# Reordering each quarter of the feed-forward groups: scaling and split first, statistics, normalisations and softmax of the other groups later

## The chip, the cores and the metric

The kernel runs on one core of a Trainium2 chip. The metric is the device time of one execution in microseconds (us). Beside it stands the span, from the first to the last instruction of one profiled execution.

Five engines work side by side, each with its own queue of instructions that it takes strictly in order: PE (TensorE, matrix products and transposes; its weight loads are listed as PEld), DVE (VectorE), ACT (ScalarE), POOL (GpSimd) and SP (SyncE, which here only issues DMAs). They wait for one another by semaphores. An instruction that waits holds up everything behind it on its own engine.

## The reference, cut to what matters

The input is 2048 tokens of 1024 numbers. Three stages follow each other; the first and the third are the feed-forward stage, with the same weights, and the middle one is a convolution with blockwise attention, which the change doesn't touch.

```
def ffn(x, weight, bias, gate_w, in_channel_scale, out_channel_scale):
    routing = softmax(x @ gate_w.T)                  # 8 experts
    in_scale = routing @ in_channel_scale
    out_scale = routing @ out_channel_scale
    return x * in_scale @ sign(weight).T * out_scale + bias

x = x + 0.5 * ffn(layernorm(x), ...)
x = x + attention(layernorm(x), ...)
x = x + 0.5 * ffn(layernorm(x), ...)
```

## The kernel before

The feed-forward stage is one function, `ffn_phase`, called twice: turn 1 (about 0 to 250 us) and turn 2 (about 905 us to the end). It takes the tokens in eight groups of 256. The body of the loop is run once per group g, and is cut into four quarters q = 0 to 3; each quarter makes one 128x512 tile of the group's output. Each engine has its own body, written out by hand, and in it work of several groups is interleaved:

- Group g itself: PE makes the product with the signed weights, sixteen matmuls a quarter (L638, `product`, two halves of eight), and the output scale (L626, `out_scale`); ACT copies the output scale (L543); DVE multiplies product and scale into y (L469, called the output multiply here); POOL adds residual and bias (L267, L270).
- Group g+1, two of its eight chunks k a quarter: PE makes the input scale of a chunk (L621, `in_scale`), DVE multiplies it with the transposed tokens (L343, `scale`), ACT rounds the result to its high part (L504, `high`), DVE subtracts to get the low part (L348, `low`). There are only two PSUM banks for these chunks, so the `in_scale` of chunk k waits for the `low` of chunk k-2. In a quarter, PE's second `in_scale` stands between the two halves of the product. In quarter 0 the first one is followed by the logits.
- Group g+2: logits (L597) and their way back (L604) in quarter 0, softmax on DVE (L319 to L336) with its exponential on ACT (L495) in quarter 1, its transposition on PE (L610, `routing`) and copy on ACT (L499) in quarter 3.
- Group g+3: statistics on DVE (L296 to L305, `stats`), the inverse root on POOL (L241, `power`) and the normalisation on DVE (L310, `normalise`) in quarter 0; its four transposes on PE (L587) in quarters 1, 2, 3 and 3, with copies on ACT (L487).
- Group g-1, in turn 1 only: statistics of its output on DVE (L356 to L365, `out_stats`) and the inverse root on POOL (L263) in quarter 0, normalisation on DVE (L371, `out_normalise`) in quarter 2, and in quarter 3 four rounds of transposes on PE (L654, `normed`) and copies on ACT (L516, `copy_normed`), which share one PSUM bank and so take turns.

In quarter 0, DVE before does the statistics of g+3 and of g-1, then the two scalings and the first split of g+1, then the normalisation of g+3, then the output multiply. Groups 0 and 5 to 7 are special: group 0 has no g-1; groups 5 to 7 have no g+3; groups 6 and 7 have no g+2; in group 7 of turn 1 POOL and DVE also prepare filters of the convolution (L785, L792).

Of the kernel before, what the change touches and what calls it, by code (L numbers as in the profile page):

```python
# [13 lines left out]
ALU = mybir.AluOpType  # L14
# [58 lines left out]
def exists(g):  # L73

    return not isinstance(g, int) or 0 <= g < NG
# [5 lines left out]
def ffn_phase(nc, sems, set_up, turn, src, dst, w_t, bias, gate_t, ics, ocs, ident, X, conv):  # L81
# [33 lines left out]
    with ExitStack() as ctx:  # L115
# [55 lines left out]
        with nc.Block() as block:  # L171
# [58 lines left out]
            def _(pool):  # L230
# [27 lines left out]
                def body(g, p):  # L258
                    if exists(g + 3):
                        power(g + 3)  # L260
                    if X is not None and exists(g - 1):
                        pool.wait_ge(n_var, g)
                        pool.tensor_tensor(nrstd[:], nvpe[:], minus_half[:], ALU.pow).then_inc(n_rstd, 1)  # L263
                    for q in range(4):
                        t, h = q // 2, slice(q % 2 * HALF, q % 2 * HALF + HALF)
                        pool.wait_ge(res_loaded[t], 16 * g + 16)
                        pool.tensor_tensor(res[:, t, h], res[:, t, h], hbias[:, h], ALU.add).then_inc(res_biased, 1)  # L267
                        pool.wait_ge(res_biased, 4 * g + q + 1)
                        pool.wait_ge(m_scaled, 4 * g + q + 1)
                        pool.tensor_tensor(y[:, p, t, h], y[:, p, t, h], res[:, t, h], ALU.add).then_inc(y_done, 1)  # L270
                        if q == 3 and X is not None and exists(g - 1) and not late(g):
                            differences(g - 1)
                        if q == 0 and X is not None and late(g):
                            conv.outer_sum(pool, 0)
                            conv.outer_sum(pool, 1)
                        if q >= 2 and X is not None and late(g):
                            t = q - 2
                            pool.wait_ge(n_var, NG + t)
                            pool.tensor_tensor(nrstd[:, t:t + 1], nvpe[:, t:t + 1], minus_half[:, t:t + 1], ALU.pow).then_inc(n_rstd, 1)
# [4 lines left out]
            def _(dve):  # L284
# [148 lines left out]

                def body(g, p):
                    for q in range(4):
                        if q == 0 and exists(g + 3):
                            stats(g + 3, 1 - p)
                        if q == 0 and X is not None and exists(g - 1):
                            out_stats(g - 1, 1 - p)
                        if exists(g + 1):  # L440
                            scale(g + 1, 1 - p, 2 * q)
                            if q:
# [1 line left out]
                            scale(g + 1, 1 - p, 2 * q + 1)  # L444
                            low(g + 1, 1 - p, 2 * q)
                        if q == 0 and exists(g + 3):
                            normalise(g + 3, 1 - p)
                        if q == 1 and exists(g + 2):
                            softmax(g + 2)
                        if q == 2 and X is not None and exists(g - 1):  # L450
                            out_normalise(g - 1, 1 - p)
                        if q == 3 and exists(g + 1):
                            low(g + 1, 1 - p, KD - 1)
                        if q == 2 and X is not None and late(g):
# [26 lines left out]
            def _(act):  # L481
# [15 lines left out]
                def copy_routing(g, p):  # L497
                    act.wait_ge(r_full, g + 1)
                    act.copy(rT[:, p, :], p_r[:, 0:FTOK]).then_inc(r_copied, 1)  # L499
# [39 lines left out]
                def body(g, p):  # L539
                    for q in range(4):  # L540
# [5 lines left out]
                        if q == 0 and X is not None and late(g):  # L546
                            conv.outer_scale(act, 0)
                            conv.outer_scale(act, 1)
                        if q == 3 and exists(g + 2):
                            copy_routing(g + 2, p)  # L550
                        if q == 0 and exists(g + 2):
                            copy_logits(g + 2)
                        if exists(g + 1):
                            high(g + 1, 1 - p, 2 * q)
                        if q == 3 and X is not None and exists(g - 1):
                            copy_normed(g - 1, 0)
                            copy_normed(g - 1, 1)
                        if exists(g + 1):
                            high(g + 1, 1 - p, 2 * q + 1)
                        if q == 3 and X is not None and exists(g - 1):  # L560
                            copy_normed(g - 1, 2)
                            copy_normed(g - 1, 3)
                        if q == 1 and exists(g + 2):
                            exponent(g + 2)
                        if exists(g + 3):
                            for piece in PIECES[q]:
# [8 lines left out]
            def _(pe):  # L575
# [99 lines left out]
                def body(g, p):  # L675
                    for q in range(4):
# [7 lines left out]
                            routing(1)  # L684
                        if exists(g + 1):
                            in_scale(g + 1, 1 - p, 2 * q)
                        if q == 3 and exists(g + 2):
                            routing(g + 2)
                        if q == 0 and exists(g + 2):
                            logits(g + 2, p)  # L690
                        if q == 3 and X is not None and exists(g - 1):
                            for c in range(4):
                                normed(g - 1, 1 - p, c)
                                product(g, p, q, 2 * c, 2 * c + 2)
                                if c == 1 and exists(g + 1):
                                    in_scale(g + 1, 1 - p, 2 * q + 1)
                                if c == 1 and exists(g + 3):
                                    transposes(g + 3, 1 - p, 2)
                        else:
                            if not first:  # L700
                                product(g, p, q, 0, 4)
                            if exists(g + 1):
                                in_scale(g + 1, 1 - p, 2 * q + 1)
                            if q == 3 and exists(g + 3):
# [978 lines left out]
```

## Time and profile before

| | |
|---|---|
| device time, median of 3 runs | 1110.57 us (1109.88 to 1112.51) |
| the profiled execution, its own time | 1117.16 us |
| its span | 1115.4 us |
| PE busy | 952.7 us, 85% |
| DVE busy | 718.2 us, 64% |
| ACT busy | 452.8 us, 41% |
| POOL busy | 371.6 us, 33% |

In the page, busy shares are means over the whole span. The stages differ, so the timeline (every instruction in order of its start, with the engine's idle time before it and what released it) and the table by stretches are what tells about the feed-forward groups.

### The profile page before, as it was taken

What the parts mean: (1) busy time and instruction counts of PE and PEld (TensorE: products, weight loads), DVE (VectorE), ACT (ScalarE), POOL (GpSimd) and SP (SyncE); (2) the same over time, 40 slices, a digit from 0 to 9 for tenths busy, and PEclk for the clock granted to TensorE, in tenths of its full rate; (3) what the DMA queues carried; (4) which work ended last, traced back from release to release, by engine and by line L of the source; (5) the groups of instructions that cost most, each with busy time, mean ns of one, the idle gap of its engine ahead of it and who ended that gap; (6) DMA issues with size and microseconds to landing.
All of it is one profiled execution on the core that took longest, in us unless ns stands there. A gap on an engine that the chain in (4) does not pass through costs nothing. (4 is left out here: it accounts for less than half of the span.)

```text
span 1115.4 us, 15622 instructions
## 1 busy us (share of the span) xinstructions
PE 952.7 (85%) x4960; PEld 716.4 (64%) x4960; DVE 718.2 (64%) x1469; ACT 452.8 (41%) x1127; POOL 371.6 (33%) x305
## 2 busy tenths in 40 slices
PE   4898888868898998967978996998799746999997
PEld 3576666653335876845766785886678634678786
DVE  6677775477998885532774587288458447576652
ACT  3534444431244352323763454356345305433431
POOL 2245555564542200000223131133214411355555
PEclk9799999988999999986988997998899885999999
DMA  8333322322323426533002112121101258154243
GB/s 280 127 133 114 113 75 76 132 95 85 113 94 135 168 66 245 207 133 113 2 19 76 39 57 76 38 75 65 48 38 58 95 165 279 58 189 149 78 132 113
DMA packets 44781, 121.45 MB, mean 109 GB/s; under 512 B 5936, under 2 KB 18224, under 8 KB 43312
## 3 DMA queue, kind: packets, MB, share of 16 engines
q1 hardware_dynamic: 44720, 120.68, 31.4%
q8 instruction: 33, 0.54, 0.2%
q14 instruction: 28, 0.23, 0.1%
HBM read 89.21 MB, written 31.46 MB: 108 GB/s over the span
## 5 line engine op out<-in xcount | busy, mean ns | idle before, releaser
L638 PE MATMUL f_p_m<-f_wsign,f_a_hi 128*128 128x512 f32 x512 | 209.0, 408 | 0.0
L638 PE MATMUL f_p_m<-f_wsign,f_a_lo 128*128 128x512 f32 x512 | 203.1, 397 | 0.0
L1342 POOL TENSOR_TENSOR a_s<-a_s,a_sums 128x512 f32<-128x512 f32 x64 | 66.6, 1041 | 252.7 <-DVE a_sums L1481 252.7
L270 POOL TENSOR_TENSOR f_y<-f_y,f_res 128x512 f32<-128x512 f32 x64 | 82.7, 1293 | 147.3 <-DVE f_y L469 147.1
L1549 PE MATMUL a_p_g<-a_xs_hi,x_room 128*128 128x512 f32 x256 | 102.4, 448 | 22.8 <-DVE a_xs_lo L1433 22.2
L1397 ACT ACTIVATE a_s<-a_s,a_nmx 128x128 f32<-128x128 f32 x256 | 99.3, 390 | 39.1 <-DVE a_nmx L1477 39.0
L638 PEld LDWEIGHTS f_p_m<-f_wsign,f_a_hi 128*128 128x128 f32 x512 | 97.6, 191 | 22.6 <-issue 4.1
L638 PEld LDWEIGHTS f_p_m<-f_wsign,f_a_lo 128*128 128x128 f32 x512 | 97.7, 191 | 16.8
L1114 PE MATMUL c_p_m<-c_vf,c_ring_f 128*128 128x512 f32 x192 | 86.8, 609 | 9.5 <-DVE c_ring_f L792 6.4
L343 DVE TENSOR_TENSOR f_p_s<-f_xT,f_p_s 128x256 f32<-128x256 f32 x120 | 50.2, 424 | 65.9 <-PE f_p_s L621 65.2
L504 ACT CAST f_a_hi<-f_p_s 128x256 fp32r<-128x256 f32 x120 | 44.5, 376 | 107.1 <-DVE f_p_s L343 106.3
L1116 PE MATMUL c_p_m<-c_vh,c_ring 128*128 128x512 f32 x192 | 76.8, 400 | 8.7 <-DVE c_ring L1000 6.9
L267 POOL TENSOR_TENSOR f_res<-f_res,f_hbias 128x512 f32<-128x512 f32 x64 | 83.3, 1302 | 0.0
L1549 PEld LDWEIGHTS a_p_g<-a_xs_hi,x_room 128*128 128x128 f32 x256 | 53.0, 207 | 39.3 <-DVE a_xs_lo L1433 21.3
L469 DVE TENSOR_TENSOR f_y<-f_p_m,f_oscale 128x512 f32<-128x512 f32 x64 | 43.9, 686 | 51.3 <-PE f_p_m L638 51.3
L1117 PE MATMUL c_p_m<-c_vl,c_ring 128*128 128x512 f32 x192 | 76.0, 396 | 0.0
L1118 PE MATMUL c_p_m<-c_vh,c_ring 128*128 128x512 f32 x192 | 75.9, 396 | 0.0
L1114 PEld LDWEIGHTS c_p_m<-c_vf,c_ring_f 128*128 128x128 f32 x192 | 36.8, 195 | 59.1 <-issue 52.2
L487 ACT COPY f_xT<-f_p_t 128x512 f32<-128x512 f32 x56 | 33.1, 592 | 82.6 <-PE f_p_t L587 82.6
L587 PE MATMUL f_p_t<-ident,f_xin 128*128 128x128 f32 x224 | 38.6, 300 | 31.0 <-DVE f_xin L310 26.2
L785 POOL TENSOR_TENSOR c_raw<-c_raw 128x512 f32<-128x512 f32 x24 | 35.7, 1491 | 73.0 <-DMA c_raw<-in_conv_w_dram 48.8
L1472 DVE TENSOR_TENSOR a_s<-a_p_s,a_mask 128x512 f32<-128x512 f32 x64 | 43.7, 683 | 20.9 <-PE a_p_s L1573 20.8
(178 smaller groups left out, 2066.5 us busy)
## 6 DMA issues: line engine op xcount, KB each, us to landing
c_raw<-in_conv_w_dram SPq DMA_DIRECT2D x24, 768.0 KB, 4.3
f_y<-in_w_t_dram SPq DMA_DIRECT2D x16, 512.0 KB, 7.9
f_res<-in_x_dram SPq DMA_DIRECT2D x16, 512.0 KB, 3.8
x_after_ffn<-f_y SPq DMA_DIRECT2D x8, 1024.0 KB, 6.0
f_res<-x_after_attention SPq DMA_DIRECT2D x16, 512.0 KB, 3.9
out_dram<-f_y SPq DMA_DIRECT2D x8, 1024.0 KB, 6.1
f_xin<-in_x_dram SPq DMA_DIRECT2D x7, 1024.0 KB, 7.6
a_residual<-x_after_ffn SPq DMA_DIRECT2D x14, 512.0 KB, 3.5
```

The costliest lines, as they stand in the source:

```text
L267: pool.tensor_tensor(res[:, t, h], res[:, t, h], hbias[:, h], ALU.add).then_inc(res_biased, 1)
L270: pool.tensor_tensor(y[:, p, t, h], y[:, p, t, h], res[:, t, h], ALU.add).then_inc(y_done, 1)
L343: dve.tensor_tensor(bank[:, FTOK:HALF], xT[:, p, k, :], bank[:, 0:FTOK], ALU.mult).then_inc(scaled, 1)
L504: act.copy(a_hi[:, p, k, :], scale_bank(g, k)[:, FTOK:HALF]).then_inc(hi_done, 1)
L638: last = pe.matmul(p_m[:, q % 2, :], part[:, p, k, q // 2 * P:q // 2 * P + P], wsign[:, k, q % 2 * HALF:q % 2 * HALF + HALF], start=(k == ...
L1114: last = pe.matmul(out, ring_f[:, slot, 0, cols], vf[:, f, k, :], start=start, stop=stop)
L1116: pe.matmul(out, ring[:, slot, 0, cols], vh[:, f, k, :], start=start, stop=False)
L1117: pe.matmul(out, ring[:, slot, 0, cols], vl[:, f, k, :], start=False, stop=False)
L1118: last = pe.matmul(out, ring[:, slot, 1, cols], vh[:, f, k, :], start=False, stop=stop)
L1342: pool.tensor_tensor(s[:, r], s[:, r], sums[:, r].unsqueeze(2).broadcast_to([P, 4, P]), ALU.mult).then_inc(probs_ready, 1)
L1397: done = act.activation(s[:, r, h, :], s[:, r, h, :], ACT.Exp, bias=nmx[:, r, h:h + 1], scale=SCALE, accum_out=sums[:, r, h:h + 1])
L1549: mm = pe.matmul(p_g[:, bank, :], a, b, start=n == 0, stop=n == len(pairs) - 1)
```

## The change

The work stays the same; only its order in the loop's body changes, on four engines.

- DVE: in quarter 0 the scaling and split of g+1 come first, then the statistics of g+3. The normalisation of g+3 and then the output statistics of g-1 come in quarter 1. The softmax of g+2 comes in quarter 2, behind the output normalisation of g-1.
- POOL: the inverse root for g-1 comes at the start of quarter 1 instead of ahead of quarter 0.
- ACT: the exponential comes in quarter 2 instead of 1; in quarter 3 the copy of the routing comes behind the first `high` and the first `copy_normed`.
- PE: in quarter 3 the transposition of the routing comes behind the first round of `normed` and product (in turn 2 behind the first half of the product).

```
@@ POOL
                 def body(g, p):
                     if exists(g + 3):
                         power(g + 3)
-                    if X is not None and exists(g - 1):
-                        pool.wait_ge(n_var, g)
-                        pool.tensor_tensor(nrstd[:], nvpe[:], minus_half[:], ALU.pow).then_inc(n_rstd, 1)
                     for q in range(4):
+                        if q == 1 and X is not None and exists(g - 1):
+                            pool.wait_ge(n_var, g)
+                            pool.tensor_tensor(nrstd[:], nvpe[:], minus_half[:], ALU.pow).then_inc(n_rstd, 1)
@@ DVE
                     for q in range(4):
-                        if q == 0 and exists(g + 3):
-                            stats(g + 3, 1 - p)
-                        if q == 0 and X is not None and exists(g - 1):
-                            out_stats(g - 1, 1 - p)
                         if exists(g + 1):
                             scale(g + 1, 1 - p, 2 * q)
                             if q:
                                 low(g + 1, 1 - p, 2 * q - 1)
                             scale(g + 1, 1 - p, 2 * q + 1)
                             low(g + 1, 1 - p, 2 * q)
                         if q == 0 and exists(g + 3):
+                            stats(g + 3, 1 - p)
+                        if q == 1 and exists(g + 3):
                             normalise(g + 3, 1 - p)
-                        if q == 1 and exists(g + 2):
-                            softmax(g + 2)
+                        if q == 1 and X is not None and exists(g - 1):
+                            out_stats(g - 1, 1 - p)
                         if q == 2 and X is not None and exists(g - 1):
                             out_normalise(g - 1, 1 - p)
+                        if q == 2 and exists(g + 2):
+                            softmax(g + 2)
@@ ACT
-                        if q == 3 and exists(g + 2):
-                            copy_routing(g + 2, p)
                         if q == 0 and exists(g + 2):
                             copy_logits(g + 2)
                         if exists(g + 1):
                             high(g + 1, 1 - p, 2 * q)
                         if q == 3 and X is not None and exists(g - 1):
                             copy_normed(g - 1, 0)
+                        if q == 3 and exists(g + 2):
+                            copy_routing(g + 2, p)
+                        if q == 3 and X is not None and exists(g - 1):
                             copy_normed(g - 1, 1)
...
-                        if q == 1 and exists(g + 2):
+                        if q == 2 and exists(g + 2):
                             exponent(g + 2)
@@ PE
                             in_scale(g + 1, 1 - p, 2 * q)
-                        if q == 3 and exists(g + 2):
-                            routing(g + 2)
...
                             for c in range(4):
                                 normed(g - 1, 1 - p, c)
                                 product(g, p, q, 2 * c, 2 * c + 2)
+                                if c == 0 and exists(g + 2):
+                                    routing(g + 2)
...
                                 product(g, p, q, 0, 4)
+                            if q == 3 and exists(g + 2):
+                                routing(g + 2)
```

## Rows read from the trace of the kernel before

**Rows 1.** Busy time by stretch: group 2 of turn 1, group 1 of turn 2.
```profile
core 0: us, PE busy (x) PEld busy (x) DVE busy (x) ACT busy (x) POOL busy (x), PEclk, DMA share, GB/s
91.85:119.60 27.75, 23.50 (x130) 17.74 (x130) 19.96 (x51) 12.07 (x24) 14.00 (x13) 1.00 0.31 115
975.00:995.80 20.80, 20.36 (x114) 16.40 (x114) 14.55 (x41) 8.13 (x21) 10.98 (x10) 1.00 0.43 153
```
**Rows 2.** Timeline of PE, turn 1, group 2: start, busy, [idle before, releaser].
```profile
91.85 1.07 PE L597 MATMUL f_p_r<-f_xT,f_gateT 128*32 128x256 f32 x16 [0.40 <-ACT f_xT L487]
...
98.72 0.38 PE L621 MATMUL f_p_s<-f_rT,f_ics 128*128 128x256 f32 x1 [1.11 <-DVE f_a_lo L348]
...
101.85 0.39 PE L621 MATMUL f_p_s<-f_rT,f_ics 128*128 128x256 f32 x1 [0.93 <-DVE f_a_lo L348]
```
**Rows 3.** Timeline of DVE in the same group, the same columns.
```profile
90.33 2.46 DVE L296 BATCH_NORM_STATS2 f_st<-f_xin 128x6 f32<-128x512 f32 x4
...
93.14 1.22 DVE L305 TENSOR_SCALAR f_vpe<-f_mv 128x2 f32<-128x2 f32 x1
94.28 2.46 DVE L356 BATCH_NORM_STATS2 f_nst<-f_y 128x6 f32<-128x512 f32 x4
...
100.46 0.68 DVE L469 TENSOR_TENSOR f_y<-f_p_m,f_oscale 128x512 f32<-128x512 f32 x1
101.06 0.41 DVE L343 TENSOR_TENSOR f_p_s<-f_xT,f_p_s 128x256 f32<-128x256 f32 x1
101.39 0.41 DVE L348 TENSOR_TENSOR f_a_lo<-f_p_s,f_a_hi 128x256 fp32r<-128x256 f32 x1
...
102.95 0.16 DVE L319 TENSOR_REDUCE f_r_max<-f_p_r 128x2 f32<-128x16 f32 x1
...
104.75 0.68 DVE L469 TENSOR_TENSOR f_y<-f_p_m,f_oscale 128x512 f32<-128x512 f32 x1
```
**Rows 4.** Timeline of ACT in the same group: a high part, then quarter 3.
```profile
101.51 0.37 ACT L504 CAST f_a_hi<-f_p_s 128x256 fp32r<-128x256 f32 x1 [2.62 <-DVE f_p_s L343]
...
110.45 0.40 ACT L504 CAST f_a_hi<-f_p_s 128x256 fp32r<-128x256 f32 x1
110.72 1.11 ACT L516 COPY X<-f_p_n 128x512 f32 x1
```
**Rows 5.** Timeline of PE, turn 2, group 1.
```profile
975.06 1.07 PE L597 MATMUL f_p_r<-f_xT,f_gateT 128*32 128x256 f32 x16 [0.33 <-ACT f_xT L487]
...
982.64 0.28 PE L621 MATMUL f_p_s<-f_rT,f_ics 128*128 128x256 f32 x1
...
984.61 0.60 PE L587 MATMUL f_p_t<-ident,f_xin 128*128 128x128 f32 x4
```
**Rows 6.** Timeline of DVE in the same group of turn 2.
```profile
978.35 0.43 DVE L343 TENSOR_TENSOR f_p_s<-f_xT,f_p_s 128x256 f32<-128x256 f32 x1 [0.39 <-PE f_p_s L621]
...
979.02 1.85 DVE L310 TENSOR_SCALAR f_xin<-f_xin,f_mv,f_rstd 128x1024 f32<-128x1024 f32 x2
```
**Rows 7.** Timeline of POOL in the same group of turn 2.
```profile
977.65 0.70 POOL L241 TENSOR_TENSOR f_rstd<-f_vpe,f_minus_half 128x2 f32<-128x2 f32 x1 [1.55 <-DVE f_vpe L305]
978.32 1.29 POOL L267 TENSOR_TENSOR f_res<-f_res,f_hbias 128x512 f32<-128x512 f32 x1
```
**Rows 8.** Timelines of DVE and PE, turn 1, group 0.
```profile
47.97 1.53 DVE L310 TENSOR_SCALAR f_xin<-f_xin,f_mv,f_rstd 128x1024 f32<-128x1024 f32 x2
...
52.93 0.60 PE L587 MATMUL f_p_t<-ident,f_xin 128*128 128x128 f32 x4
```
**Rows 9.** Timelines of PE, ACT and POOL, turn 1, groups 5, 6 and 7.
```profile
174.95 1.07 PE L597 MATMUL f_p_r<-f_xT,f_gateT 128*32 128x256 f32 x16 [0.40 <-ACT f_xT L487]
...
197.56 0.40 PE L626 MATMUL f_p_o<-f_ocs,f_rT 128*128 128x512 f32 x1
...
191.19 1.08 ACT L516 COPY X<-f_p_n 128x512 f32<-128x512 f32 x1
...
214.36 1.07 ACT L516 COPY X<-f_p_n 128x512 f32<-128x512 f32 x1
...
229.45 3.00 POOL L785 TENSOR_TENSOR c_raw<-c_raw 128x512 f32<-128x512 f32 x2
```

More of the change, by code:

```diff
@@ L260, in body @@
                         power(g + 3)
-                    if X is not None and exists(g - 1):
-                        pool.wait_ge(n_var, g)
-                        pool.tensor_tensor(nrstd[:], nvpe[:], minus_half[:], ALU.pow).then_inc(n_rstd, 1)
                     for q in range(4):
+                        if q == 1 and X is not None and exists(g - 1):
+                            pool.wait_ge(n_var, g)
+                            pool.tensor_tensor(nrstd[:], nvpe[:], minus_half[:], ALU.pow).then_inc(n_rstd, 1)
                         t, h = q // 2, slice(q % 2 * HALF, q % 2 * HALF + HALF)
@@ L435, in body @@
                     for q in range(4):
[L436 to L439, printed above, removed]
                         if exists(g + 1):
@@ L446, in body @@
                         if q == 0 and exists(g + 3):
+                            stats(g + 3, 1 - p)
+                        if q == 1 and exists(g + 3):
                             normalise(g + 3, 1 - p)
-                        if q == 1 and exists(g + 2):
-                            softmax(g + 2)
+                        if q == 1 and X is not None and exists(g - 1):
+                            out_stats(g - 1, 1 - p)
                         if q == 2 and X is not None and exists(g - 1):
                             out_normalise(g - 1, 1 - p)
+                        if q == 2 and exists(g + 2):
+                            softmax(g + 2)
                         if q == 3 and exists(g + 1):
@@ L548, in body @@
                             conv.outer_scale(act, 1)
-                        if q == 3 and exists(g + 2):
-                            copy_routing(g + 2, p)
                         if q == 0 and exists(g + 2):
@@ L556, in body @@
                             copy_normed(g - 1, 0)
+                        if q == 3 and exists(g + 2):
+                            copy_routing(g + 2, p)
+                        if q == 3 and X is not None and exists(g - 1):
                             copy_normed(g - 1, 1)
@@ L562, in body @@
                             copy_normed(g - 1, 3)
-                        if q == 1 and exists(g + 2):
+                        if q == 2 and exists(g + 2):
                             exponent(g + 2)
@@ L686, in body @@
                             in_scale(g + 1, 1 - p, 2 * q)
-                        if q == 3 and exists(g + 2):
-                            routing(g + 2)
                         if q == 0 and exists(g + 2):
@@ L694, in body @@
                                 product(g, p, q, 2 * c, 2 * c + 2)
+                                if c == 0 and exists(g + 2):
+                                    routing(g + 2)
                                 if c == 1 and exists(g + 1):
@@ L701, in body @@
                                 product(g, p, q, 0, 4)
+                            if q == 3 and exists(g + 2):
+                                routing(g + 2)
                             if exists(g + 1):
```

## The prediction

> **What bounds the kernel now.** I read the table by stretches first, because the shares of the page mix three stages. In turn 2 a full group takes 20.8 us, and PE is busy for 20.36 of them: PE is the bound, and nothing but PE's own work can make these groups shorter [rows 1]. A full group of turn 1 takes 27.75 us with 23.50 us of PE, so some 4 us of PE are idle there [rows 1]. The timeline of PE says where: the `in_scale` of chunks 2 and 3 wait 1.11 and 0.93 us for a `low` of DVE [rows 2], and the rest lies in quarter 3, where the rounds of `normed` and `copy_normed` take turns on one bank. The timeline of DVE shows the cause of the first two waits: DVE does both statistics ahead of the scalings [rows 3]. These 2.04 us a group are what the change goes after. But it also has a price, and to find it I follow DVE through the new order, instruction by instruction.
>
> **Durations.** From start to next start on DVE [rows 3]: output multiply 0.60, a scaling 0.33 (and the same for a `low`), softmax 1.80 (102.95 to 104.75). Statistics: 2.81 to their last instruction (90.33 to 93.14), and that one takes 0.17 when nothing holds it (an estimate from the short rows; 1.22 is with a hold, below), so 2.94. From the start of a `low` to the `in_scale` that waits for it 0.46 (101.39 to 101.85) [rows 2, 3]; from the start of an `in_scale` to the scaling behind it 0.32 (the one at 978.03 to 978.35) [rows 6]. From a scaling to its high part 0.46 (101.06 to 101.51) and from that to `copy_normed` 0.27 [rows 3, 4]. A normalisation is two instructions; 1.44 from start to next start when POOL is still, busy 1.53 [rows 8].
>
> **The hold by POOL.** The same two instructions are busy for 1.85 us when they start at 979.02, while a POOL add runs from 978.32 to 979.61 [rows 6, 7]. The rest of the add was 0.59, the normalisation got 0.32 longer: it pays the rest of the POOL instruction less some 0.25. The last statistics instruction at 93.14, 1.22 long, shows the same [rows 3]. In the new order, POOL's inverse root starts 0.25 after the last statistics instruction and its two adds follow at once, so that the normalisation meets the second add with some 0.93 to go: I take 0.68 more, 2.12 in all. The ends are 1.44 (POOL still) and 2.4 (the whole rest of the add). The Trainium skill says of this in SBUF — State Buffer, "Who interferes with whom", that a two-port VectorE operation and a GpSimd one exclude each other for a whole instruction, and the later fully blocks. By that rule alone each normalisation costs the whole rest, which is 0.25 more; the sum would be about 3 us longer. The trace agrees in kind, and the row pays a bit less.
>
> **Turn 2, full groups (1 to 4), time t from the start of the logits, 975.06** [rows 5]. DVE scales chunk 0 at once, but the `in_scale` of chunk 1 stands on PE behind the logits and half a product, so DVE stands idle until t = 3.29 [rows 5, 6]. Before, the statistics filled that time. Now: scaling 3.29, `low` 3.62, statistics 3.95, output multiply 6.89, scaling 7.49, `low` 7.82, and so the `in_scale` of chunk 3 at 8.28, where it stands at 982.64, t = 7.58, today: 0.70 lost [rows 5]. Scaling 8.60, `low` 8.93, normalisation of g+3 at 9.26, done at 11.38. PE's transposes of g+3 wait for just that and start at 11.45; today at 984.61, t = 9.55 [rows 5]. So 1.90 us a group (0.70 is part of it). Behind that, the softmax in quarter 2 fits: its result is wanted only after half of quarter 3's product, and nothing else gets late. What this group had covered at nothing, DVE's statistics under PE's logits and half product, is now in the open. 4 groups by 1.90: 7.6 us. Bounds by the normalisation's length: 1.2 to 2.2 a group.
>
> **Turn 1, full groups (1 to 4), t from 91.85** [rows 2]. The two waits of 1.11 and 0.93 change: the first goes, since `low` of chunk 0 is done by 4.0; the second becomes the 0.70 above. The normalisation runs as above from 9.24 to 11.38, and holds the transposes. Then come the output statistics of g-1, 2.92, and only then, at 14.30, the output multiply of quarter 1. Queued behind it: scaling 14.90, `low` 15.23, `in_scale` of chunk 5 at 15.69 (PE could do it at 13.8), scaling 16.01, `low` 16.34, output normalisation 16.67. Its inverse root on POOL, now behind quarter 0's adds, is done at 15.1 and not late, but POOL's next adds hold it for 0.7: to 18.80. Softmax to 20.60, output multiply, scaling of chunk 6 at 21.20, its high part 21.66, first `copy_normed` 21.93. Today that copy starts at 110.72, t = 18.87 [rows 4]. From there on the rounds run as before, each waiting for the last, to the group's end; `routing` (ready at 20.6) and its copy, now inside the rounds, fall into waits that are there anyway and cost nothing; without that cover the copy would cost about 0.4 on ACT. So a group gets 3.06 longer, 4 by that: 12.2 us. With the holds at today's size it is 2.4, with none 1.7, with the whole rests 3.6.
>
> **The other groups.** Group 0 of each turn: the statistics that today run while DVE has nothing to do come at 47.97, then 2.94 + 0.60 + 0.33 + 0.33, `in_scale` and the next two (0.13 + 0.32 + 0.33 + 0.33 behind the last `low`), normalisation from 53.28 to 55.40, transposes at 55.46 for 52.93 [rows 8]: 2.5 each, 5.0. Group 5 of turn 1: no statistics of g+3, but the chain over output statistics, output normalisation and softmax gives the first copy at t = 19.1 for 16.24 (191.19 less 174.95) [rows 9]: 2.9. Group 6 has no softmax and today starves for the late statistics: first copy 16.1 after its start for 16.80 (214.36 less 197.56) [rows 9]: a gain of 0.7. Group 7: the inverse root gets behind the filter's outer sum on POOL, 3.00 us [rows 9], so the normalisation runs after it and not beside it: between 0 and 3.0 later, less the hold that it is spared; I take 1.4. Groups 5 to 7 of turn 2: nothing, their DVE has slack. No DMA moves; the loads of tokens and of the residual are issued on PE's and POOL's progress and have many us to spare.
>
> **The sum.** Turn 1: 2.5 + 12.2 + 2.9 - 0.7 + 1.4 = 18.3; turn 2: 2.5 + 7.6 = 10.1; together 28.4 us. The profiled execution took 1117.2 us with its 1.8 us around the span, and would take 1145.6; it stands 6.6 above the median of the runs, which are the measure: 1110.6 + 28.4 = 1139.0. With the least of all bounds (no holds, group 7 for nothing) the sum is some 16, with the largest 34: 1127 to 1145.
>
> **The rivals.**
> - Faster: the waits for `low` go and nothing takes their place, because DVE (19.96 of 27.75 us busy [rows 1]) finds room for the moved work in the idle time of later quarters. It is decided at the transposes of g+3 in quarter 1: if the normalisation ended before PE comes to them (t = 9.55), this would be it. Gain 4 by 2.04, and 2.1 in group 6: 1100. Against it: DVE's queue is in order, and the chain above is 1.8 us late at that very point. For it: only the mean share of DVE. 6 in 100.
> - Turn 1 comes out even: the 2.04 a group won at the first waits pay for what comes later, if quarter 3's rounds of copies had slack to take up the late start. Then only turn 2 and the group 0s lose, 1110.6 + 10 to 12: 1121. Against it: the copies are a chain without slack, and the first starts 0.27 behind the high part [rows 4]. 8 in 100.
> - No effect (within 0.3%), because losses and gains meet, or because the order has no influence on the end of a group: 1110.6. Against it: PE's 20.36 of 20.8 us in turn 2 leave no slack to hide 1.9 us in [rows 1]. 4 in 100.
> - More than the sum: the longer gaps on PE (up to 1.9 us at one place, some 7 us in a group) pull down its granted clock, which is 1.00 in these groups today [rows 1]. A few us of each of nine groups at the lower of its two levels, 1.2 GHz, would add some 10 us: 1149. 8 in 100.
>
> **How the numbers follow.** The forecast's case has 74 in 100, own range 1127 to 1145. Slower by over 0.3% (about what a measurement of this kernel can tell from no change) are the forecast, the even turn 1 and the clock: 0.90. Faster 0.06, same 0.04. For 8 in 10 the range goes from 1121 to 1146.
>
> **What would show it right or wrong.** In the trace of the changed kernel: DVE idle for about 3 us between the first two scalings of quarter 0; transposes of g+3 waiting for L310 by 1 to 1.9 us in turn 2, in groups of 22.7 us; in turn 1 the `in_scale` of chunk 5 waiting for a `low` by some 1.7 us, a first L516 about 22 us behind the logits, groups of 30.8 us. It is wrong if PE doesn't wait at the transposes of quarter 1, if L310 or L371 is much off 2.1 us, or if PE's clock falls below 1.00 in these groups.

## The result, and the profile after

The changed kernel takes 1158.94 us (median of 4 runs, 1155.98 to 1165.69), the kernel before 1110.66 in the same comparison: 1.0441 times as long, interval 1.0393 to 1.0489. That is 48 us more where 28.4 were forecast, so the direction was right and the time lies outside the range. The profiled execution took 1165.69 us with a span of 1163.9, against the span of 1115.4 before. It stands 6.7 above its median, as the one before did (6.6), so the two traces can be compared directly: 48.5 us between them.

First the parts of the page (span; busy time, share and instructions of each engine) that answer to the table of before:

```profile
span 1163.9 us, 15618 instructions
PE 963.5 (83%) x4960; PEld 720.8 (62%) x4960; DVE 734.5 (63%) x1469; ACT 453.1 (39%) x1127; POOL 375.8 (32%) x305
```

The work is the same, yet DVE is busy for 16 us more and PE for 11 us more. Both are instructions that got longer: DVE's mostly because POOL holds them (the normalisations L310 and L371 alone make 16 us), PE's in the main because its granted clock is lower in places. The rest of the 48 us is idle time.

The table by stretches shows the groups that answer to [rows 1]: groups 2 and 3 of turn 1, group 1 of turn 2. Its columns are those of [rows 1].

```profile
core 0: us, PE busy (x) PEld busy (x) DVE busy (x) ACT busy (x) POOL busy (x), PEclk, DMA share, GB/s
102.20:135.20 33.00, 25.47 (x134) 19.02 (x136) 20.41 (x51) 12.13 (x24) 14.42 (x13) 0.95 0.27 96
135.20:167.00 31.80, 23.87 (x130) 17.46 (x130) 20.64 (x51) 12.08 (x24) 14.36 (x13) 1.00 0.28 99
1011.00:1035.00 24.00, 20.86 (x118) 16.24 (x118) 15.74 (x41) 8.12 (x20) 11.39 (x10) 1.00 0.38 132
```

A group of turn 2 goes from 20.8 to 24.0 us with nearly the same PE work: nearly all of it is idle time. A group of turn 1 goes from 27.75 to between 31.9 and 33.4, and the difference within these is the clock: the one at 1.00 has 23.87 us of PE, the one at 0.95 has 25.47.

Taken from logits to logits, the whole account of the two traces is (us):

| | forecast | measured |
|---|---|---|
| group 0, turn 1 and turn 2 | +2.5 and +2.5 | +5.5 and +5.4 |
| groups 1 to 4, turn 1 | +12.2 | +20.4 |
| groups 5, 6, 7, turn 1 | +2.9, -0.7, +1.4 | +4.0, +0.4, +0.5 |
| groups 1 to 4, turn 2 | +7.6 | +12.7 |
| all else (start -0.8, middle stage -0.7, set-up of turn 2 +1.3, end -0.2) | 0 | -0.4 |
| sum | 28.4 | 48.5 |

**Where the forecast's chain shows.** The timeline of DVE in group 2 of turn 1 (start, busy, [idle before, releaser]), with the five places that the prediction named:

```profile
105.44 0.43 DVE L343 TENSOR_TENSOR f_p_s<-f_xT,f_p_s 128x256 f32<-128x256 f32 x1 [3.19 <-PE f_p_s L622]
...
106.11 2.46 DVE L296 BATCH_NORM_STATS2 f_st<-f_xin 128x6 f32<-128x512 f32 x4
...
111.68 2.08 DVE L310 TENSOR_SCALAR f_xin<-f_xin,f_mv,f_rstd 128x1024 f32<-128x1024 f32 x2
113.68 2.46 DVE L356 BATCH_NORM_STATS2 f_nst<-f_y 128x6 f32<-128x512 f32 x4
...
119.17 3.12 DVE L371 TENSOR_SCALAR f_y<-f_y,f_nmv,f_nrstd 128x1024 f32<-128x1024 f32 x2
```

And PE in the same group (lines on PE stand one higher than before), from its waits:

```profile
110.59 0.39 PE L622 MATMUL f_p_s<-f_rT,f_ics 128*128 128x256 f32 x1 [0.69 <-DVE f_a_lo L348]
...
113.89 0.65 PE L588 MATMUL f_p_t<-ident,f_xin 128*128 128x128 f32 x4 [1.09 <-DVE f_xin L310]
...
118.07 0.39 PE L622 MATMUL f_p_s<-f_rT,f_ics 128*128 128x256 f32 x1 [1.32 <-DVE f_a_lo L348]
...
122.34 0.66 PE L655 MATMUL f_p_n<-ident,f_y 128*128 128x128 f32 x4 [1.28 <-DVE f_y L371]
...
126.56 0.63 PE L655 MATMUL f_p_n<-ident,f_y 128*128 128x128 f32 x4 [1.97 <-ACT X L516]
```

DVE stands idle for 3.19 us between the first two scalings, with the statistics, which used to fill this time, queued behind. Then everything comes late, in the order forecast: `in_scale` of chunk 3 by 0.7, the transposes of g+3, `in_scale` of chunk 5, the first round of `normed`.

**The first thing that the forecast missed: two adds, not one.** Turn 2, group 1, DVE and then POOL:

```profile
1020.60 2.99 DVE L310 TENSOR_SCALAR f_xin<-f_xin,f_mv,f_rstd 128x1024 f32<-128x1024 f32 x2
```

```profile
1020.07 1.29 POOL L270 TENSOR_TENSOR f_y<-f_y,f_res 128x512 f32<-128x512 f32 x1
1021.33 1.70 POOL L267 TENSOR_TENSOR f_res<-f_res,f_hbias 128x512 f32<-128x512 f32 x1
```

The normalisation is two instructions. The first meets the add of quarter 0 (L270), which runs until 1021.36. POOL then starts the add of the residual for quarter 1 (L267) at once, so the second instruction meets that one as well. The pair takes 2.99 us; it is 1.53 on a still POOL [rows 8] and was 1.85 with one add [rows 6, 7]. The add itself takes 1.70 for its usual 1.29, so the two engines hold each other. The Trainium skill (SBUF — State Buffer, "Who interferes with whom") gives the rule that a VectorE instruction in a two-port mode and a GpSimd one exclude each other for a whole instruction, whoever comes first. The trace agrees in kind, and the rule has to be applied to each instruction of a pair. In size it pays less: the rest of the first add (0.76), half a pair (0.76), a whole add (1.29) and the other half (0.76) would make some 3.6 us by that rule, an estimate, where the pair took 2.99.

PE's transposes wait for just this:

```profile
1023.72 0.65 PE L588 MATMUL f_p_t<-ident,f_xin 128*128 128x128 f32 x4 [1.99 <-DVE f_xin L310]
```

They start at t = 12.70 (counted from the logits, 1011.02), where 11.45 was forecast and 9.55 was before.

**The second: the granted clock.** The table by stretches over the end of group 2 of turn 1, and over group 0 (start, length; the granted clock is the third number from the end):

```profile
122.00:126.00 4.00, 2.02 (x10) 1.27 (x10) 2.91 (x14) 2.17 (x5) 1.16 (x1) 1.00 0.22 88
126.00:130.00 4.00, 3.44 (x18) 3.25 (x19) 1.18 (x3) 2.08 (x4) 1.33 (x2) 0.73 0.00 0
130.00:135.00 5.00, 4.20 (x19) 2.81 (x18) 0.71 (x2) 3.06 (x4) 1.11 (x1) 0.87 0.00 2
52.00:56.00 4.00, 2.60 (x9) 1.55 (x8) 4.00 (x5) 0.37 (x1) 3.18 (x3) 0.60 0.00 0
56.00:60.00 4.00, 4.00 (x13) 3.38 (x14) 1.16 (x3) 1.46 (x3) 2.51 (x2) 0.55 0.23 72
```

Behind PE's gaps of 1.28 and 1.97 us the clock falls from its upper level, 2.4 GHz, to the lower, 1.2 GHz, for part of the next four us (mean 0.73; read us by us it is 0.50 from 128 to 131) and is back at 1.00 by 132. The rounds of `normed` and product run through just this stretch. ACT's copies tell what that costs:

```profile
125.34 1.07 ACT L516 COPY X<-f_p_n 128x512 f32 x1
...
127.31 1.08 ACT L516 COPY X<-f_p_n 128x512 f32 x1 [0.69 <-PE f_p_n L655]
...
130.25 1.09 ACT L516 COPY X<-f_p_n 128x512 f32 x1 [0.96 <-PE f_p_n L655]
```

One round takes 1.97 us (125.34 to 127.31), the next 2.94 (127.31 to 130.25). Some 1.1 us a group is lost so, in three of the four full groups of turn 1; the fourth kept 1.00. In group 0, where the waits are 1.96 and 1.40 us, the clock is 0.55 to 0.60 over eight us.

The length of the waits alone doesn't decide it. Group 1 and group 3 of turn 1 have the same ones, to 0.01 us; the clock fell in group 1 and stayed at 1.00 in group 3:

```profile
88.99 0.65 PE L655 MATMUL f_p_n<-ident,f_y 128*128 128x128 f32 x4 [1.35 <-DVE f_y L371]
...
93.03 0.66 PE L655 MATMUL f_p_n<-ident,f_y 128*128 128x128 f32 x4 [1.87 <-ACT X L516]
...
155.41 0.65 PE L655 MATMUL f_p_n<-ident,f_y 128*128 128x128 f32 x4 [1.36 <-DVE f_y L371]
...
159.45 0.66 PE L655 MATMUL f_p_n<-ident,f_y 128*128 128x128 f32 x4 [1.87 <-ACT X L516]
```

```profile
92.00:96.00 4.00, 2.97 (x13) 2.63 (x14) 0.50 (x2) 2.31 (x5) 1.91 (x2) 0.72 0.02 4
159.00:163.00 4.00, 3.50 (x21) 2.79 (x21) 1.18 (x3) 2.91 (x5) 1.33 (x2) 1.00 0.00 0
```

### The profile page after: what moved, and what is told of

It is laid out like the page before. It is cut to its first block and busy times, and to the rows that moved or that the text cites. A ratio compares the mean times of both kernels' runs of the same rounds, so it can differ in the third digit from the quotient of the medians.

```text
span 1163.9 us, 15618 instructions
## 1 busy us (share of the span) xinstructions
PE 963.5 (83%) x4960; PEld 720.8 (62%) x4960; DVE 734.5 (63%) x1469; ACT 453.1 (39%) x1127; POOL 375.8 (32%) x305
## 5 line engine op out<-in xcount | busy, mean ns | idle before, releaser
L639 PE MATMUL f_p_m<-f_wsign,f_a_hi 128*128 128x512 f32 x512 | 212.6, 415 | 0.0
L639 PE MATMUL f_p_m<-f_wsign,f_a_lo 128*128 128x512 f32 x512 | 206.9, 404 | 0.0
L270 POOL TENSOR_TENSOR f_y<-f_y,f_res 128x512 f32<-128x512 f32 x64 | 82.5, 1290 | 125.6 <-DVE f_y L469 124.1
L639 PEld LDWEIGHTS f_p_m<-f_wsign,f_a_hi 128*128 128x128 f32 x512 | 100.2, 196 | 23.3 <-issue 4.1
L267 POOL TENSOR_TENSOR f_res<-f_res,f_hbias 128x512 f32<-128x512 f32 x64 | 87.7, 1370 | 0.0
L588 PEld LDWEIGHTS f_p_t<-ident,f_xin 128*128 128x128 f32 x224 | 29.8, 159 | 60.8 <-DVE f_xin L310 32.5
```

The lines of the kernel that those rows point to most:

```text
L588: last = pe.transpose(bank[:, c * FTOK + t * P:c * FTOK + t * P + P], xin[:, p, t, k * P:k * P + P], ident[:])
L639: last = pe.matmul(p_m[:, q % 2, :], part[:, p, k, q // 2 * P:q // 2 * P + P], wsign[:, k, q % 2 * HALF:q % 2 * HALF + HALF], start=(k == ...
```

## The experiments

Each experiment's time is followed by its ratio to the kernel before, with the interval. In the sessions of the experiments the median of the kernel before was 1113.7 to 1113.8 us, 3 us above the 1110.66 measured beside the changed kernel, so ratios are compared, not microseconds. The changed kernel's ratio of 1.0441 makes 49 us of 1110.66. Group lengths are from the profiled executions (from logits to logits).

### Which of the three moved steps costs most

Three kernels undo one move of the changed kernel each.

**u1_stats_first**: the statistics of g+3 first again in quarter 0; all else as changed.

```
 for q in range(4):
+    if q == 0 and exists(g + 3):
+        stats(g + 3, 1 - p)
     ...
-    if q == 0 and exists(g + 3):
-        stats(g + 3, 1 - p)
```

> The changed kernel with one move undone: the statistics of g+3 stand ahead of the scalings of quarter 0 again. Theory (DVE's order: work that had run while PE held back the second in_scale is now in the open, and POOL's adds hold the normalisations): the second in_scale of quarter 1 no longer waits, the transposes of g+3 in turn 2 wait under 1 us instead of 2, turn 2 groups 21.5 us for 23.95, turn 1 groups 30.8 for about 32.8; 1132 us. Rival (the place of softmax and exponential is what costs): the time stays within 5 us of the changed kernel's 1159.

Measured: 1134.05 us, 1.0192 (1.0158 to 1.0225). Groups of turn 2 take 21.7 us, group 0 of turn 2 is back at 18.2, as before; those of turn 1 take 30.4 to 32.0. By stretches, group 1 of turn 1 and group 1 of turn 2:

```profile
62.62:94.58 31.96, 25.31 (x131) 18.99 (x131) 21.03 (x53) 12.20 (x24) 13.01 (x12) 0.95 0.28 99
988.35:1010.07 21.72, 20.57 (x115) 16.28 (x115) 14.43 (x41) 8.19 (x20) 10.97 (x10) 1.00 0.42 146
```

Undoing this one move gives back 28 of the 49 us (1.0441 less 1.0192, times 1110.66). With the statistics in the time in which DVE must wait for PE, POOL's inverse root and adds are early, the normalisation meets none of them to speak of (L310 has a mean of 0.83 us for one, 1.66 a pair), and the transposes wait 0.75 us instead of 1.99. The clock of both group 0s is back at 1.00. So the 28 us are not the uncovered statistics alone: the holds on L310 and the low clock of group 0, which the move had brought with it, go as well. The output normalisation still meets two adds here (3.12 us).

**u2_outstats_first**: the output statistics of g-1, and POOL's inverse root with them, back first in quarter 0; the statistics of g+3 stay late.

```
 for q in range(4):
+    if q == 0 and X is not None and exists(g - 1):
+        out_stats(g - 1, 1 - p)
     ...
-    if q == 1 and X is not None and exists(g - 1):
-        out_stats(g - 1, 1 - p)
```

> The changed kernel with the output statistics of g-1 and POOL's inverse root for them back in quarter 0, ahead of the scalings. Theory: turn 2 as in the changed kernel (groups 23.95 us); in turn 1 the chain of DVE in quarter 1 loses 2.9 us of work, so its groups come to 28.3 us; 1137 us. It shows how much of turn 1 hangs on quarter 1. Rival (softmax's place): no change in turn 1, 1159.

Measured: 1151.01 us, 1.0322 (1.0297 to 1.0347), 14 us more than expected (9 by the ratio). Three full groups of turn 1 by stretches:

```profile
102.43:132.07 29.64, 23.58 (x130) 17.74 (x131) 19.42 (x50) 12.02 (x24) 14.88 (x13) 1.00 0.29 107
68.28:102.43 34.15, 27.85 (x130) 20.81 (x130) 19.45 (x50) 12.04 (x24) 13.36 (x12) 0.85 0.26 93
132.07:163.27 31.20, 25.06 (x130) 19.05 (x131) 19.43 (x50) 12.03 (x24) 14.90 (x13) 0.95 0.28 101
```

The same instructions take 29.64, 31.20 or 34.15 us as the clock is 1.00, 0.95 or 0.85. I had expected 28.3. So 1.3 us are missing at a clock of 1.00, and the rest of the miss in these groups is the clock. The trace shows where part of the 1.3 arises, though no run isolates it: the transposes of g+3 start at t = 12.54 for 11.71 in the changed kernel. The output statistics, now first, wait for POOL's last add and put the statistics of g+3 0.4 us later (t = 4.34 for 3.93), and L310 takes 2.48 us for 2.08, since POOL no longer waits for `out_stats` between its adds.

**u3_softmax_q1**: the softmax and its exponential back in quarter 1.

```
-    if q == 2 and exists(g + 2):
-        softmax(g + 2)
+    if q == 1 and exists(g + 2):
+        softmax(g + 2)
...
```

> The changed kernel with softmax and exponential back in quarter 1 (behind the output statistics). Theory: in turn 1 the chain up to the first copy of quarter 3 has the same length, no gain; in turn 2 the in_scale of chunk 5 gets late by 0.5 us, groups 24.4 us; 1161 us. Rival (softmax in quarter 2 delays quarter 3): turn 1 falls to near its old time, 1140 us or less.

Measured: 1165.21 us, 1.0459 (1.0439 to 1.048); groups of turn 2 take 24.4 us for 23.95 (the last one 25.5, at a clock of 0.93), those of turn 1 32.7 to 33.6. The time can't be told from the changed kernel's (1.0441, 1.0393 to 1.0489), so the place of the softmax is not what costs: undoing this move gives nothing back, and in turn 2 it makes a group 0.4 us longer. Of the three moves it is the one that does no harm.

### POOL's hold

**g1_pool_gate**: as changed, but POOL doesn't start its add of y in quarter 0 (and 1) before DVE has done the normalisation of the inputs (and of the outputs).

```
     pool.tensor_tensor(res[:, t, h], res[:, t, h], hbias[:, h], ALU.add).then_inc(res_biased, 1)
+    if q == 0 and exists(g + 3):
+        pool.wait_ge(x_normed, g + 4)
+    if q == 1 and X is not None and exists(g - 1):
+        pool.wait_ge(y_normed, g + 1)
```

> The changed kernel, but POOL waits with its adds to y of quarters 0 and 1 until DVE has done the normalisation (of g+3 and of g-1), so that no POOL add runs beside one. Theory (POOL's adds hold the normalisations, two adds for one normalisation, 1.6 us each where it is 3.0 to 3.1 long): L310 and L371 pairs fall to 1.5 us; turn 2 groups from 23.95 to 22.0 us, turn 1 groups to 29.4, and if the clock then stays at 1.00 in all of them, 1128 us; if the clock falls as now, 1132. Rival (the adds are needed early and the length of the pairs is memory traffic of DMAs): pairs stay at about 3 us and the time doesn't fall.

Measured: 1148.95 us, 1.0298 (1.0264 to 1.0331). Both pairs are at 1.53, and a group of turn 2 takes 22.5 us for 23.95: the hold cost 1.5 us there, and the order alone costs 1.7. But the groups of turn 1 hardly move, 32.1 to 33.2 us at a clock of 0.90 to 0.95, and the time is 17 to 21 us above the expected one (12 to 16 by the ratio). The timeline of DVE in such a group, and then of POOL, says why:

```profile
149.50 1.53 DVE L375 TENSOR_SCALAR f_y<-f_y,f_nmv,f_nrstd 128x1024 f32<-128x1024 f32 x2
...
152.46 1.19 DVE L335 CAST f_r_hi<-f_r_exp 128x16 fp32r<-128x16 f32 x1
```

```profile
151.11 1.29 POOL L274 TENSOR_TENSOR f_y<-f_y,f_res 128x512 f32<-128x512 f32 x1 [2.09 <-DVE f_y L375]
152.36 1.27 POOL L267 TENSOR_TENSOR f_res<-f_res,f_hbias 128x512 f32<-128x512 f32 x1
```

The adds that were put off now meet the softmax. Its cast of 16 numbers a partition, 0.17 us in the changed kernel, takes 1.19, and the product ahead of it 0.42 for 0.17. The two normalisations are 2.1 us shorter together, the softmax 1.3 longer, and none of the four groups kept a clock of 1.00, where one had. In turn 1 the hold has in good part been moved, not taken away.

**g2_gate_softmax**: the same, and POOL's adds of quarters 1 and 2 wait for the softmax too.

```
+    if q == 2 and exists(g + 2):
+        pool.wait_ge(routing_ready, g + 3)
     pool.tensor_tensor(res[:, t, h], res[:, t, h], hbias[:, h], ALU.add).then_inc(res_biased, 1)
     ...
+    if q == 1 and X is not None and exists(g + 2):
+        pool.wait_ge(routing_ready, g + 3)
```

> The changed kernel with the gates on POOL of the earlier run (adds to y of quarters 0 and 1 wait for the normalisations), and here the adds of quarters 1 and 2 wait for the softmax too, since the earlier run showed softmax's small casts held for 1.2 us. Theory (one chain on DVE, lengthened by each POOL add that it meets): first copy of quarter 3 at 21.1 us behind the logits for 22.3, groups 1.2 shorter than with the first gates, 31.0 us with the clock falling as it does, 1144 us. Rival (with the gates something else is the last to arrive): no change against the earlier gated kernel's 1149.

Measured: 1136.3 us, 1.0204 (1.0173 to 1.0235). Groups of turn 1 take 31.05, 31.32 and 31.36 us at a clock of 0.95 and 29.84 at 1.00; those of turn 2 stay at 22.5. With the softmax freed as well, all gates together give back 26 of the 49 us (1.0441 less 1.0204 is 0.0237, times 1110.7), against some 21 us by which the sixteen held normalisations of groups 0 to 6 exceed their 1.53 in the changed kernel. In the full groups and group 0s of the two traces it is 18.3 us: 7.7 in turn 1, 6.0 in turn 2, 4.6 in the two group 0s. Part of that is the clock, since group 0 is at 0.92 here for 0.86. The profiled execution is the longest of the five, 7 us above their median; its groups have the lengths expected (31.0), so that the median lies 8 us below the expected 1144 (11 by the ratio) isn't explained by them.

### The clock

**f1_filler**: as changed, with matmuls put into PE's gaps whose result is overwritten before anything reads it: 4 ahead of the transposes in quarter 1, 7 behind the first round of quarter 3.

```
+def filler(g, p, piece, n):
+    pe.wait_ge(t_copied, 4 * g + piece)
+    for _ in range(n):
+        pe.matmul(p_t[:], a_hi[:, 1 - p, 0, 0:P], wsign[:, 0, 0:HALF], start=True, stop=True)
     ...
+                if c == 0 and exists(g + 3):
+                    filler(g + 3, 1 - p, 2, 7)
     ...
+        if q == 1 and exists(g + 3):
+            filler(g + 3, 1 - p, 0, 4)
```

> The changed kernel with matmuls put on PE into two of its gaps, that write to the unused bank p_t and are overwritten: four ahead of the transposes of g+3 in quarter 1 (0.9 us), seven behind the routing's transposition in quarter 3 of turn 1 (1.6 us, where PE waits 1.9 us for the first copy). Theory (behind the gaps PE runs at the lower clock, which costs 1.1 us in three of the four full groups of turn 1 and some 2 us in group 0 of each turn): the granted clock stays at 1.00, the groups of 33.0 and 33.4 us come to 31.9, 1152 us. Rival (the lower clock has another cause, or costs nothing on the path): groups keep their lengths or get longer by the matmuls, 1159 us or more.

Measured: 1155.28 us, 1.0378 (1.0346 to 1.041), whose interval overlaps a little with the changed kernel's; the evidence is in the groups. Those of turn 1 are 31.88 to 32.03 us, all at 1.00:

```profile
69.17:101.11 31.94, 26.50 (x142) 19.46 (x142) 20.62 (x51) 12.15 (x24) 13.02 (x12) 1.00 0.28 100
101.11:133.14 32.03, 26.62 (x142) 19.56 (x142) 20.49 (x51) 12.13 (x24) 14.47 (x13) 1.00 0.28 99
```

PE does eleven matmuls more in a group and the group gets 1 to 1.5 us shorter than those that ran at 0.95. So the low clock is a cause and not just a companion of the waits, and 31.9 us is the length of a group with the order and the holds but without it. That a clock of 1.00 in four of four is no luck is shown by all traces together: in the changed kernel, u1, u2, u3, g1 and g2, 19 of the 24 full groups of turn 1 have a clock of 0.85 to 0.95; in f1 and in g3 below, with the added matmuls, none of eight. Group 0 went from 23.75 to 22.22, with a clock of 0.92 still: there it had fallen ahead of the added matmuls.

**g3_gates_and_filler**: g2 with the 7 matmuls of quarter 3.

> The changed kernel with all gates on POOL (normalisations and softmax meet no add) and with the seven filling matmuls in the gap of quarter 3, so that both things that the step sum left out are taken away together. Theory (order on DVE, plus holds, plus clock, and nothing else): full groups of turn 1 are all 29.85 us at a clock of 1.00, those of turn 2 22.45; 1132 us. Rival (something else makes the difference between the sum of the steps and the changed kernel): groups of turn 1 stay above 31 us, or the time above 1136.

Measured: 1136.35 us, 1.0193 (1.0156 to 1.0231). The groups of turn 1:

```profile
68.68:98.51 29.83, 25.39 (x137) 18.78 (x137) 18.50 (x51) 12.15 (x24) 12.55 (x12) 1.00 0.29 107
98.51:128.39 29.88, 25.44 (x137) 18.87 (x137) 18.31 (x51) 12.15 (x24) 14.02 (x13) 1.00 0.30 106
```

Each group has the length expected, to 0.1 us, but the median can't be told from that of g2: 1.0193 and 1.0204 overlap. Three groups are 1.2 to 1.6 us shorter than in g2's profiled execution, which was a long one; one trace is not the median here. By the letter the rival's "above 1136" came true, by 0.35 us; by the ratio the time is 1132 us, as expected, and the session's kernel before stood 3 us high. With both causes out of the full groups, turn 1 stands at 29.85 and turn 2 at 22.5. What is left over the kernel before, about 2.1 and 1.7 us a group, is the order itself. In the whole time the order, with the low clock that stays in group 0 (21.3 us for 18.25), makes 21 of the 49 us; holds and clock together make the other 28 (1.0441 less 1.0193).

### Is there a better order?

The changed kernel's idea, later steps for the output chain, was tried on the kernel before, where the statistics of g+3 stay at the head of quarter 0. In the code, `late(g)` is true for group 7 alone.

**p0_softmax_late**: the kernel before, turn 1 only: output statistics (and POOL's inverse root) to quarter 1, softmax and exponential to quarter 3, `routing` behind the third round.

```
     if q == 0 and exists(g + 3):
         stats(g + 3, 1 - p)
-    if q == 0 and X is not None and exists(g - 1):
+    if q == 0 and X is not None and late(g):
         out_stats(g - 1, 1 - p)
     ...
+    if q == 3 and X is not None and exists(g + 2):
+        softmax(g + 2)
     ...
-    if q == 1 and exists(g + 2):
+    if q == 1 and X is None and exists(g + 2):
         softmax(g + 2)
+    if q == 1 and X is not None and exists(g - 1) and not late(g):
+        out_stats(g - 1, 1 - p)
```

> The kernel before, with another order in turn 1 only: the statistics of g+3 stay first in quarter 0 (they fill the time in which PE holds back the second in_scale), its normalisation stays in quarter 0; the output statistics of g-1 go to quarter 1, softmax and exponential to quarter 3, the routing's transposition behind the third round there. Theory (what sets a group is the length of DVE's chain up to the scaling of chunk 6, from the second in_scale on): the two waits of 2.0 us go, the output normalisation meets two POOL adds (3.1 us), the first copy comes at 18.3 us, groups 27.2 us for 27.75, 1107 us. Rival (moving the statistics behind the split is harmful by itself): slower than the kernel before.

Measured: 1115.36 us, 1.001 (0.9988 to 1.0032). The groups have the length expected (27.10 to 27.28 us), but group 0 takes 19.97 us for 18.25, since its `routing` has no rounds to hide in and waits 1.52 us for the softmax. The four groups win 2.1 us together, group 0 loses 1.7, and 1107 us was not reached.

**p1_softmax_late_gate**: p0, and POOL's add of y in quarter 1 waits for the output normalisation.

```
+    if q == 1 and X is not None and exists(g - 1) and not late(g):
+        pool.wait_ge(y_normed, g + 1)
```

> As the run before it, and POOL's add to y of quarter 1 waits for the output normalisation. Theory: that normalisation takes 1.5 us for 3.1, first copy at 16.7 us behind the logits, groups of turn 1 25.6 us for 27.75, 1098 us. Rival (POOL becomes late by the gate): no better than the run before it.

Measured: 1110.22 us, 0.9971 (0.9952 to 0.9991); groups of 26.7 us where 25.6 were expected, and a time 0.3% below the kernel before where 1098 us was expected. DVE in such a group:

```profile
111.29 1.10 DVE L330 TENSOR_TENSOR f_r_exp<-f_r_exp,f_r_max 128x16 f32<-128x16 f32 x1
112.42 1.20 DVE L333 CAST f_r_hi<-f_r_exp 128x16 fp32r<-128x16 f32 x1
```

It is g1's lesson once more: the softmax, now late, meets the adds that the gate put off. Behind it came the scaling of chunk 7, and on ACT its high part stood ahead of the third copy, 114.71.

**p2_better_order**: p1 with the third `copy_normed` ahead of that high part on ACT, and with group 0's softmax back in quarter 1.

```
     copy_normed(g - 1, 1)
+    copy_normed(g - 1, 2)
     if exists(g + 1):
         high(g + 1, 1 - p, 2 * q + 1)
     ...
-    copy_normed(g - 1, 2)
     copy_normed(g - 1, 3)
```

> The kernel before with another order in turn 1 only (statistics of g+3 first, output statistics in quarter 1, softmax in quarter 3, POOL's add to y of quarter 1 behind the output normalisation), as in the run that gave groups of 26.75 us, with two repairs: ACT does the third copy of quarter 3 ahead of the second high part (it had stood 1.0 us behind a scaling that waited for the softmax), and group 0 keeps its softmax in quarter 1 (its routing had waited 1.5 us). Theory: groups of 25.8 us for 27.75, group 0 18.25, 1104 us against 1111 to 1114 for the kernel before. Rival (the lengths of the groups at quarter 3 are set by the rounds of copies alone): no better than 1110.

Measured: 1103.27 us (median of 6, 1099.73 to 1106.74), 0.9903 (0.9871 to 0.9935): 1% below the kernel before, clear of the interval, and well below the changed one.

```profile
65.56:91.28 25.72, 23.07 (x130) 17.79 (x130) 21.52 (x53) 11.88 (x24) 12.59 (x12) 1.00 0.35 124
91.28:117.14 25.86, 23.23 (x131) 17.91 (x131) 21.50 (x51) 11.92 (x24) 14.04 (x13) 1.00 0.35 123
```

Four groups of 25.7 to 25.9 us for 27.7 make 7.8 us; the ratio's 10.8 (interval 7.2 to 14.3) has room for that. The two repairs were made together, so their shares are not told apart. DVE is busy for 21.50 us in such a group, longer than before, because the softmax is held (its product took 1.06 us, its cast 1.21), but at a place where nobody waits for it yet. Turn 2 is as before, 20.76 a group.

## Why the prediction was right and where it failed

**Right: the bound, and what the statistics covered.** PE has no slack in turn 2 [rows 1], and DVE's queue waits for PE's second `in_scale` for some 3 us, which only the statistics filled. DVE's idle time is 3.19 us at that place, `in_scale` of chunk 3 waits 0.69 to 0.74 for a forecast of 0.70, and undoing this one move (u1) gives back 28 us, the holds and the clock that hang on it included. The rival that it comes out faster falls at the very place that it named: the transposes of g+3 wait, 1.09 us in turn 1 and 1.99 in turn 2.

**Right: turn 1's chain.** Output statistics in quarter 1, the late `low` and the late output normalisation delay the first copy as followed step by step: forecast t = 21.93, measured 23.16 (125.34 less 102.18). Early rounds had no slack to give back, so "turn 1 comes out even" falls. At the clock's upper level the full group is 31.88 for a forecast of 30.8.

**Failed: the hold's term.** "I take 0.68 more, 2.12 in all. The ends are 1.44 (POOL still) and 2.4 (the whole rest of the add)." The step let the normalisation meet one add only. It meets two, one for each of its instructions, in group 0, in turn 2 and at the output normalisation: 3.19, 2.99 and 3.12 us. Even the upper bound was too low, since it was the rest of one instruction of POOL and not of what is queued behind it. Only turn 1's L310 came out near the forecast, at 2.04 to 2.08, because POOL then has to wait for `out_stats` between its adds. Beyond the forecast's 2.12 that is 0.9 us in each full group of turn 2, 1.0 in each of the four groups and in groups 5 and 6 of turn 1, and 1.1 in each group 0: some 11.6 of the 20 us missed.

**Failed, by little: the durations around it.** L310 starts at t = 9.58 in turn 2 where 9.26 was forecast, and L371 at 16.99 in turn 1 for 16.67. Statistics to output multiply take 3.11 us for 2.94, and from the `in_scale` of chunk 3 to its scaling it is 0.43 for 0.32. So the order alone, which the forecast had at 1.2 us a group in turn 2 with POOL still, costs 1.7 (g1). With the hold this makes t = 12.70 for 11.45, the 5.1 us missed in turn 2; over all groups it is some 2.4 us (what is left of 14.0 beside the 11.6).

**Failed: the clock as an 8% rival.** "The longer gaps on PE [...] pull down its granted clock". The mechanism and the size were written down (some 10 us), but taken as unlikely. Before, PE's waits of 1.11 and 0.93 us [rows 2] went with a clock of 1.00 and that was read as safe; in the changed kernel the waits stand closer and are longer, 1.28 and 1.97 with 0.23 between, in a stretch where PE is busy for 2.02 of 4 us. They make the fall likely and not certain, as group 3 shows. It cost 3.8 us in three groups (33.44, 32.98 and 33.01 less 31.88 each) and some 1.8 in each group 0 (what is left of 5.5 beside the forecast's 2.5 and the longer hold): about 7.4. f1 takes most of that away in its trace; its ratio is 0.0063 lower, 7 us, at intervals that overlap a little. As the hold and the clock came together (the hold lengthens the very gaps), they were not two independent chances, and the top of the range, which took them one by one, was too low.

**Small terms.** Group 7 paid 0.5 for a forecast of 1.4; group 6 lost 0.4 where a gain of 0.7 was forecast, because its output normalisation is held as well. Group 5 lost 4.0 for 2.9, which is the same hold and start. The set-up of turn 2 is 1.3 us longer in this one trace, behind a DMA that landed later, and the middle stage 0.7 shorter; neither was followed up. That "no DMA moves" costs nothing stands. So 11.6, 2.4 and 7.4, less 0.9 (group 7) and 0.4 (all else), are the 20.1 us missed.

**Left open.** What makes up the whole of the 1.3 us by which u2's groups at a clock of 1.00 are longer than worked out, why two groups with the same waits differ in the clock, and how often the clock falls in a given group from one execution to the next.

## What to carry to other kernels

In a hand-written order an engine with idle time may still have none to spare at one place: look for the instruction at which it waits for another engine and keep there the work that nobody else waits for; here undoing that one move gave back 28 of 49 us. Price a hold between two engines by everything queued back to back on the other one, instruction against instruction, and, when you shield one step from it, ask which step inherits it. Where waits of 1 to 2 us come close together on PE, the clock belongs into the sum and not among the rivals, because it falls with the same gaps.

## What the runs showed of the hardware

- VectorE's two-instruction normalisation takes 1.53 us beside a still POOL, 1.85 to 2.08 with the end of one add, 2.98 to 3.19 with two adds back to back; the second add itself grows from 1.29 to 1.70. On a small operation the hold is far dearer in proportion: a cast of 128x16, 0.17 us, took 1.19 and 1.20, and a product of 128x16, also 0.17, took 1.10 (g1, p1).
- The granted clock fell to a mean of 0.73 over four us behind gaps of 1.28 and 1.97 us, and to 0.55 in group 0. Behind gaps of 1.35 and 1.87 us it fell to 0.72 in one group, and behind 1.36 and 1.87 it stayed at 1.00 in another. Eleven more matmuls in a group of turn 1 kept it at 1.00 in all four groups, and the group got 1.0 to 1.5 us shorter than those that ran at 0.95.
